# Cross-attention loops taken in turns of two pairs of chunks, with value projections and value products in runs of two pairs

## What is computed

```
x = x + cross_attention_0(layernorm(x), ctx)          # with relative positions
...
x = x + cross_attention_1(layernorm(x), ctx, mask)    # with a mask on the keys
# cross_attention: 16 heads of 16, 64 queries, 1601 keys
q = x @ Wq + bq;  k = ctx @ Wk + bk;  v = ctx @ Wv + bv
attn = softmax(scores(q, k) / 4)      # per head, over 1601 keys
out  = (attn @ v) @ Wo + bo
```

## Time and profile before

| | |
|---|---|
| median of 3 runs | 2634.69 us (2631.03 to 2641.21) |
| the profiled execution | 2644.9 us, span 2643.1 us |
| TensorE, mean granted clock | 0.962 of full speed |
| busy: TensorE | 2439.4 us (92%) |
| busy: VectorE / ScalarE / GpSimd | 1402.9 / 986.3 / 512.5 us |
| DMA | 39 GB/s mean |

### The profile page before, as it was taken

The page is one execution under the profiler, slowest core; times in us unless marked ns, Lnnn a source line. Parts: engine busy times, 40 slices in busy tenths (PEclk is TensorE's granted clock), DMA queues, the critical chain, the costliest instruction groups (busy, mean ns, idle before and its releaser), DMA issues. The chain is left out here.

```text
span 2643.1 us, 90979 instructions
## 1 busy us (share of the span) xinstructions
PE 2439.4 (92%) x41473; PEld 1761.7 (67%) x41473; DVE 1402.9 (53%) x2296; ACT 986.3 (37%) x1350; POOL 512.5 (19%) x488
## 2 busy tenths in 40 slices
PE   7999999999998888979999999999788899897898
PEld 3677776776777655647676767677567677776466
DVE  4454554455453562365545554554556666665568
ACT  2333333333332331234444444443433344333223
POOL 2322323323321212311111111110011111111000
PEclk8999999999998789989999999999899999999899
DMA  2111111111111322301111111120100000000200
GB/s 95 27 41 39 29 44 33 33 40 33 33 34 67 125 97 72 96 28 46 33 46 33 46 33 46 33 54 27 55 3 3 3 3 3 4 3 3 84 1 16
DMA packets 56727, 102.18 MB, mean 39 GB/s; under 512 B 10400, under 2 KB 49024, under 8 KB 55024
## 3 DMA queue, kind: packets, MB, share of 16 engines
q1 hardware_dynamic: 54448, 91.25, 11.3%
q0 software_dynamic: 1904, 5.15, 0.5%
HBM read 90.20 MB, written 9.21 MB: 38 GB/s over the span
## 5 line engine op out<-in xcount | busy, mean ns | idle before, releaser
L702 DVE TENSOR_REDUCE x_mx<-banks 128x2 f32<-128x800 f32 (+1 forms) x362 | 357.1, 990 | 420.0 <-PE banks L878 293.3
L903 PE MATMUL banks<-x_wv,x_cT 128*128 128x256 f32 (+1 forms) x1664 | 422.5, 396 | 4.6 <-DVE x_nmb L714 4.6
L792 PE MATMUL banks<-x_cT,x_wk 128*128 128x400 f32 (+1 forms) x1024 | 384.7, 518 | 8.0 <-DMA x_cT<-in_ctx 5.7
L903 PEld LDWEIGHTS banks<-x_wv,x_cT 128*128 128x128 f32 (+1 forms) x1664 | 296.6, 188 | 67.7 <-DVE x_nmb L714 5.8
L583 ACT ACTIVATE x_PT<-banks 128x2048 f32<-128x2048 f32 (+1 forms) x112 | 196.7, 1756 | 339.2 <-PE banks L942 339.2
L585 ACT ACTIVATE x_PT<-banks,x_kbs 128x1024 f32<-128x1024 f32 (+1 forms) x208 | 221.3, 1111 | 232.8 <-PE banks L942 232.8
L792 PEld LDWEIGHTS banks<-x_cT,x_wk 128*128 128x128 f32 x1024 | 189.1, 193 | 139.7 <-issue 26.5
L942 PE MATMUL banks<-x_qbd,x_kT 32*128 32x128 f32 x6656 | 247.6, 273 | 0.0
L942 PEld LDWEIGHTS banks<-x_qbd,x_kT 32*128 32x128 f32 x6656 | 244.0, 185 | 3.5
L922 PE MATMUL banks<-x_PT,x_V 128*32 128x64 f32 (+1 forms) x13312 | 234.5, 221 | 1.6 <-ACT x_PT L585 0.8
L922 PEld LDWEIGHTS banks<-x_PT,x_V 128*32 128x32 f32 (+1 forms) x13312 | 197.2, 110 | 49.8 <-issue 43.0
(11 more groups left out here) (411 smaller groups left out, 3631.6 us busy)
## 6 DMA issues: line engine op xcount, KB each, us to landing
x_cT<-in_ctx SPq DMA_DIRECT2D x96, 400.0 KB, 3.7
x_cT<-in_ctx SPq DMA_DIRECT2D x32, 401.0 KB, 3.9
e_up<-in_mo_up SPq DMA_DIRECT2D x9, 512.0 KB, 15.9
e_down<-in_mo_down SPq DMA_DIRECT2D x9, 512.0 KB, 15.8
x_mrow<-in_mask_row SPq DMA_DIRECT2D x1, 3202.0 KB, 14.2
t_w<-in_db_w SPq DMA_DIRECT2D x3, 1024.0 KB, 6.9
e_rows<-in_c_unfilled SPq DMA_DIRECT2D x1, 2967.0 KB, 13.6
e_xg<-e_rows SPq DMA_DIRECT2D x23, 129.0 KB, 2.1
```

The costliest lines, as they stand in the source:

```text
L702: dve.reduce_max(mx[:, H0[k]:H0[k] + 3:2, kb], g.PS[:, first:first + 2, 0:KBS[kb]], AXX).then_inc(max_read, 1)
L792: last = pe.matmul(PJ[pb][:, 0:KBS[k]], wk[:, c, gg, :], cT[:, (p + 1) % 2, c, KB0[k]:KB0[k] + KBS[k]], start=c == 0, stop=c == KC - 1)
L903: last = pe.matmul(PJ[pb][0:VCH[c + k], D * k:D * k + D], cT[:, p, cc, VK0[c + k]:VK0[c + k] + VCH[c + k]], wv[:, cc, :], start=cc == 0, s ...
```

## The change

The loops on TensorE and VectorE take two pairs at a time. For k = 0, 2, 4, 6 the order on TensorE is: a unit of maxima, scores of pair k, value projections of pairs k+1 and k+2, a unit, scores of pair k+1, a unit, value products of pairs k-1 and k. The three tables are replaced by `FRONT` (units ahead of scores), `BACK` (units behind the second scores of a turn) and `LAST` (one unit behind the loop, in the first attention only). Projections go to bank 0 for pairs 0, 2, 4, 6 and to bank 5, which the maxima also use, for pairs 1, 3, 5. A projection into bank 5 waits for the unit before it to be read, and the unit behind it waits for the copy out of bank 5. `V` holds eight chunks, and `PT` has three buffers in both attentions.

```diff
-        V = sb("V", [128, 6, H, 32])
-        NPT = 3 if rel else 2
+        V = sb("V", [128, 8, H, 32])
+        NPT = 3
...
-                self.V = [bank.use(0) for _ in range(0, NCH, 2)] if attend else None
+                self.V = [bank.use(k % 2) for k in range(NPAIR)] if attend else None
...
-        if mask:
-            SCORED = {2: 1, 4: 3, 6: 5, 8: 7, 10: 9}
-            PROJECTED = {0: 0, 2: 2, 4: 4, 6: 6, 8: 8}
-            VALUED = {}
-        else:
-            SCORED = {2: 1, 4: 3, 6: 6, 8: 8, 10: 10}
-            VALUED = {4: 4}
-            PROJECTED = {0: 0, 2: 2, 4: 5, 6: 7, 8: 9, 10: 11}
+        FRONT = {0: 0, 1: 1, 2: 3, 3: 4, 4: 6, 5: 7, 6: 9}
+        BACK = {1: 2, 3: 5, 5: 8} if mask else {1: 2, 3: 5, 5: 8, 6: 10}
+        LAST = () if mask else (11,)
...
+                if attend and ahead:
+                    maximum(FRONT[0])
                 if attend:
                     values(0)
...
-                for c in range(0, NCH, 2) if attend else ():
-                    if ahead and c in SCORED:
-                        maximum(SCORED[c])
-                    if ahead and c in VALUED:
-                        maximum(VALUED[c])
-                    if ahead and c in PROJECTED:
-                        maximum(PROJECTED[c])
-                    if c + 2 < NCH:
-                        values(c + 2)
+                for k in range(0, NPAIR, 2) if attend else ():
+                    if k and ahead:
+                        maximum(FRONT[k])
+                    for j in (k + 1, k + 2):
+                        if j < NPAIR:
+                            values(2 * j)
+                        if j == k + 1 and j in FRONT and ahead:
+                            maximum(FRONT[j])
+                    scored = min(k + 1, NPAIR - 1)
+                    if ahead and scored in BACK:
+                        maximum(BACK[scored])
+                for u in LAST if attend and ahead else ():
+                    maximum(u)
...
                     pb = take(bank, plan.V[c // 2])
+                    if pb and ahead:
+                        pe.wait_ge(max_read, units(b + 1) + FRONT[c // 2])
...
-                    for c in range(0, NCH, 2):
-                        scores(c)
-                        if ahead and c in SCORED:
-                            maximum(SCORED[c])
-                        for a in (c - 2, c - 1) if c else ():
-                            attend_values(a)
-                        if ahead and c in VALUED:
-                            maximum(VALUED[c])
-                        if c + 2 < NCH:
-                            project_values(c + 2)
-                        if ahead and c in PROJECTED:
-                            maximum(PROJECTED[c])
+                    for k in range(0, NPAIR, 2):
+                        if ahead:
+                            maximum(FRONT[k])
+                        scores(2 * k)
+                        for j in (k + 1, k + 2):
+                            if j < NPAIR:
+                                project_values(2 * j)
+                        if k + 1 < NPAIR:
+                            if ahead:
+                                pb, use = plan.V[k + 1]
+                                pe.wait_ge(free[pb], bank.value(pb, use))
+                                maximum(FRONT[k + 1])
+                            scores(2 * k + 2)
+                        scored = min(k + 1, NPAIR - 1)
+                        if ahead and scored in BACK:
+                            maximum(BACK[scored])
+                        for j in (k - 1, k):
+                            for a in (2 * j, 2 * j + 1) if 0 <= j < NPAIR - 1 else ():
+                                attend_values(a)
+                    for u in LAST if ahead else ():
+                        maximum(u)
```

More of the change, by code:

```diff
@@ L303, in __init__ @@
                 self.NM = bank.use(0) if attend else None
-                self.V = [bank.use(0) for _ in range(0, NCH, 2)] if attend else None
+                self.V = [bank.use(k % 2) for k in range(NPAIR)] if attend else None
                 self.WO = tail and not p
+        NPAIR = -(-NCH // 2)
         SECT, used = [], [0, 0, 0]
@@ L340, in next_keys @@
             return (Bank(base, stride, i - 1) if 0 < i < B // 2 - 1 else Bank(base)), plans[p], i, p
-        SCORED = {2: 1, 4: 4, 6: 7, 8: 10, 10: 13}
-        VALUED = {2: 2, 4: 5, 6: 8, 8: 11, 10: 14}
-        PROJECTED = {0: 0, 2: 3, 4: 6, 6: 9, 8: 12, 10: 15}
         H0 = [0, 1, 4, 5]
@@ L352, in cross_attention @@
         LOOPED = [(kb, k) for kb, k in ALL if (kb, k % 2) not in HEADED]
-        if mask:
-            SCORED = {2: 1, 4: 3, 6: 5, 8: 7, 10: 9}
-            PROJECTED = {0: 0, 2: 2, 4: 4, 6: 6, 8: 8}
-            VALUED = {}
-        else:
-            SCORED = {2: 1, 4: 3, 6: 6, 8: 8, 10: 10}
-            VALUED = {4: 4}
-            PROJECTED = {0: 0, 2: 2, 4: 5, 6: 7, 8: 9, 10: 11}
+        FRONT = {0: 0, 1: 1, 2: 3, 3: 4, 4: 6, 5: 7, 6: 9}
+        BACK = {1: 2, 3: 5, 5: 8} if mask else {1: 2, 3: 5, 5: 8, 6: 10}
+        LAST = () if mask else (11,)
+        assert sorted([*FRONT.values(), *BACK.values(), *LAST]) == list(range(len(LOOPED)))
         def cast(b, kb, gg=1):
@@ L724, in values @@
                     dve.wait_ge(full[pb], bank.value(pb, use))
-                    if later(b) or c >= 6:
-                        dve.wait_ge(av_done, NCH * b + (c - 4 if c >= 6 else 0))
+                    if later(b) or c >= 8:
+                        dve.wait_ge(av_done, NCH * b + (c - 6 if c >= 8 else 0))
                     if VCH[c] < VCH[min(c + 1, NCH - 1)]:
@@ L732, in values @@
                         return
-                    dve.tensor_copy(V[0:VCH[c], c % 6:c % 6 + n2, :, 0:HD],
+                    dve.tensor_copy(V[0:VCH[c], c % 8:c % 8 + n2, :, 0:HD],
                                     PJ[pb][0:VCH[c], 0:D * n2].rearrange("p (a h d) -> p a h d", a=n2, h=H)).then_inc(free[pb], 1)
+                if attend and ahead:
+                    maximum(FRONT[0])
                 if attend:
@@ L921, in attend_values @@
                         r = 32 * (h % 4)
-                        last = pe.matmul(OT[r:r + 32, S * (h // 4):S * (h // 4) + S], V[0:VCH[c], c % 6, h, :],
+                        last = pe.matmul(OT[r:r + 32, S * (h // 4):S * (h // 4) + S], V[0:VCH[c], c % 8, h, :],
                                          PT[0:VCH[c], c // 2 % NPT, c % 2, S * h:S * h + S], start=c == 0 and h < 4,
```

## The result

Four runs of the changed kernel gave 2697.91 us in the median (2684.95 to 2708.02); the kernel before, run beside it on the same chip, gave 2634.28. The ratio is 1.0214, with a 95% interval of 1.0184 to 1.0245: **slower by 2.1%**, and 39 us over the upper end of the predicted range. The profiled execution has a span of 2693.2 us, 50.1 more than the 2643.1 of before, and the mean granted clock is 0.959 (0.962 before).

What follows compares the result with a forecast made beforehand. TensorE was taken to bound both cross-attentions; +14.1 (first attention), -2.4 (second), -0.3, +1.1 and -1.8 (special batches) gave +10.7 us on 2634.7, so 2645.4 us, range 2631 to 2659.

Steps and rivals of the forecast that it cites:

- What bounds it, and the pieces: Both cross-attentions: TensorE bounds them, so the change works through its pieces' prices in their new places and its waits.
- A run of two projections: Value projections of two pairs side by side on TensorE: 3.66 us instead of 3.86.
- unit to unit: Successive units of maxima on TensorE: never under 1.43 us apart, since VectorE must read each first.
- Two pairs of value products and what leaves them: Two pairs in a run, followed by row-group work: 1.80 + 0.20 = 2.00 us.
- rival 1: Steps behind a released wait, such as value products to unit, cost more: +8 us, so 2653; chance 0.15.
- Rival 3: Each change of shape costs more than read, so fewer changes save more: -10 us, about 2635; chance 0.12.
- The new waits: TensorE waits for VectorE's reads, for exponentials in first turns, and at the first attention's loop end.
- The first turn's wait for ScalarE: Second attention, first turn: too little work covers the exponentials, so TensorE waits about 0.8 to 1 us.
- The end of the loop in the first attention: Unit 9 to the keys' projection: 4.34 us, bound by VectorE's reads, +2.48 us a batch.
- rival 4: First attention's loop end does not wait, units being read beside other work: -26 us, so 2619; chance 0.05.
- the sum in the first attention: Terms of one first-attention batch add to +1.01 us, over fourteen batches +14.1 us.
- Rival 2: Granted clock falls to half at the first attention's loop end: +12 to +24 us, about 2663; chance 0.08.

Runs made afterwards that it cites:

- e1: The changed kernel with context blocks 1 to 3 of a batch loaded only when the batch's last chunk is scored: 2673.14 us, ratio 1.0122.
- e4: The changed kernel with first-attention units 6 and 10 between the two pairs of value products, none directly ahead of the keys' projection: 2659.88 us, ratio 1.0070.
- e7: e4 with the late context loads of e1: 2646.86 us, ratio 1.0030.
- e9: The kernel before with the second attention's first value projection moved behind the first scores, directly ahead of the second's: 2636.77 us, ratio 0.9993.

## Why the prediction was wrong, step by step

The forecast was 2645.4 us, 10.7 above before; measured were 63.6.

*What bounds it, and the pieces: right.* A run of two projections takes 3.65 us (forecast 3.66) and unit to unit 1.44 (1.43), here of TensorE in the first turn of a masked batch:

```profile
1446.62 3.69 PE L905 MATMUL banks<-x_wv,x_cT 128*128 128x256 f32 x16
1450.24 0.34 PE L878 MATMUL banks<-x_kbf,x_qbf 32*128 32x400 bf16 x2
...
1453.20 0.34 PE L878 MATMUL banks<-x_kbf,x_qbf 32*128 32x400 bf16 x2
1453.91 0.40 PE L936 MATMUL banks<-x_nmb,x_ones 32*128 32x512 bf16 x4 [0.37 <-ACT x_PT L579]
...
1455.13 3.72 PE L905 MATMUL banks<-x_wv,x_cT 128*128 128x256 f32 x16
1458.78 0.34 PE L878 MATMUL banks<-x_kbf,x_qbf 32*128 32x400 bf16 x2
```

Two pairs of value products and what leaves them took 1.93 us (454.29 to 456.22) where I had 2.00; leaving them for a unit is not dearer than I took, so rival 1 is out. Rival 3's gain isn't seen either: the middle turn from L936 at 1453.91 to the next at 1462.52 is 8.61 us, against my 8.63.

*The new waits: right.* The first turn's wait for ScalarE is 0.71 us from the unit (1453.20 to 1453.91; I said 0.8 to 1). The end of the loop in the first attention, forecast at 4.34 us from unit 9 to the keys' projection:

```profile
363.88 0.34 PE L878 MATMUL banks<-x_kbf,x_qbf 32*128 32x400 bf16 x2
...
365.31 0.34 PE L878 MATMUL banks<-x_kbf,x_qbf 32*128 32x400 bf16 x2 [0.54 <-DVE x_mx L696]
...
366.75 0.34 PE L878 MATMUL banks<-x_kbf,x_qbf 32*128 32x400 bf16 x2
368.18 2.96 PE L792 MATMUL banks<-x_cT,x_wk 128*128 128x401 f32 x8 [1.09 <-DVE x_mx L696]
```

It is 4.30, and 14 x 1.09 = 15.3 us for the last wait alone against my 14 x 1.16. So rival 4 is out. Batches free of long stalls bear out the sum in the first attention: 49.15 and 50.99 us, for 48.28 and 49.83 before, +0.9 and +1.2 where I had +1.01.

*The step that failed* is none of the sum's terms but what was left out of it: "a run of two pairs costs 3.66", "two in a run ... 2.00". I priced each piece by its own rows and took for granted that TensorE is fed at any density of instructions. The rows that I took of before could not show it otherwise, since their longest stretch without a projection holds 208 instructions, less than one block. But its trace could, in the row of L2391. There, too, the gaps lie at equal distances: of the 42 the 35 over 0.3 us all leave 193 to 196 when their number is divided by 256. The densest part:

```profile
2413.81 0.21 PE L2391 MATMUL banks<-d_XX,d_C 64*64 64x64 f32 x1 [1.58 <-issue]
...
2417.68 0.21 PE L2391 MATMUL banks<-d_XX,d_Y 64*64 64x64 f32 x1 [1.35 <-issue]
```

Seven such edges follow from 2413.81 to 2437.97, one each 3.8 to 4.1 us, and from 2400 to 2443 the DMA moved nothing but ten instruction packets (4 GB/s):

```profile
q8 instruction: 10, 0.16, 1.4%
```

So TensorE got a block of 256 instructions about every 4.0 us there, with no load beside it. The new order wants 410 in a row in 5.2 us; at that pace they take 6.4 us, an estimate (410 / 256 x 4.0) that could have been made beforehand. It is an upper bound, since projections stand on either side. I looked at the lines that the change touches and not at the first row of the waits view; it named the effect, at the same kind of work. The missing term is the 33.5 us of "issue" (0.2 before), and with it part of the clock's. The Trainium skill, Runtime: NRT & Kernel Launch, section Instruction fetch mechanics, says that TensorE's instruction memory is refilled in blocks of 256 instructions of 16 KiB, and that the fetch is hidden behind the issue of instructions. The block size is what the trace shows (332 packets of 16 KB for 85,066 instructions); that it is hidden holds for the attentions of the kernel before, but neither for its L2391 nor for this one, and there the measurement decides.

*Rival 2, the falling clock, came in part.* The stretches at half clock in the two attentions sum to 34.2 us for 13.6 before, so some 10 us of work time was lost (half of the 20.6 more); I had given 12 to 24 us and a chance of 0.08. Of the seven new stretches two begin at the keys' projection behind the loop's end (261.6 and 473.2), as the rival said. The other five begin 0.2 to 1.1 us after TensorE goes on from a stall, and those are the five stalls of 2.0 us and more. Either is enough by itself: in e1, whose stalls are all under 1.2 us, six stretches begin at the loop's end and none behind a stall; in e4, without the wait at the loop's end, three begin behind its three longest stalls (1.6, 1.8 and 2.0 us); in e7, with neither, there is none but those that the kernel before has in the last batches.

*How the sum stands now.* In the two stretches read above, waits for other engines are 34 us (8 before) and "issue" 30 (0.2 before; some 4 us more lie ahead of the stretches); with gaps too short for the view they make the 58 us of idle time. Busy time fell by 6 in spite of some 10 us lost by the clock, so 16 us were saved, as I take it by the fewer changes of shape: that is a difference, and no run here isolates it. 58 - 6 = 52 us. Without stalls and clock 52 - 30 - 10 = 12 is left, where I had forecast +10.7. By attention it is 34 - 14 - 7 = 13 in the first, for 13.5 in the forecast, and 18 - 16 - 3 = -1 in the second, for -2.8. So the terms that I summed were right, and two that I had left out make up the other 40.

*The range* held rivals of known kinds alone. Nothing in it stood for the supply of instructions, which no row that I had taken showed at the new density.

## What to carry to other kernels

Gathering like pieces into longer runs saves changes of shape, but it also gathers short instructions; count instructions per microsecond between the long matmuls, and compare the longest stretch with one block of the instruction supply. If a piece stops inside a run of like matmuls, with "issue" as its releaser, look at the packets of kind "instruction" 1.2 to 1.6 us earlier, and test it by shifting the whole list by a few instructions. Read the first rows of the waits view of before even where they belong to other parts of the kernel: a limit that shows there can show where you are about to gather work. And before a wait is removed, ask which other wait ran beside it: it will be the next to end last (e9).

## What was not expected of the hardware

- TensorE stalled for 0.2 to 2.8 us inside runs of short fp32 matmuls at edges of its 256-instruction blocks, and, in the attentions of these kernels, nowhere else with "issue" as the releaser. It went on 1.2 to 1.6 us after an instruction packet had landed, in every one of the gaps over 0.9 us inside runs of scores, values' products and L936.
- A context load of 400 KB just ahead of the packet made the stall about 1 us longer: the longest gap in the scores was 2.3 us with the load and 1.0 without (e1). Without any load L2391 stalled for up to 2.0 us.
- A shift of 32 instructions moved the time from a ratio of 1.0214 to 1.0153. A dense kernel's time thus depends on the number of instructions ahead of its loop, and two such kernels can't be compared to 0.5% by one build each.
- No packet of before or after started more than 301 instructions ahead of the edge at which its block begins, and no block was used sooner than 1.2 us after its packet had landed. So hardly more than one block was on its way at a time. Why it isn't asked for earlier no run here settles.
- That it takes a stretch of more than one block was seen in few orders only (208, about 410, split, and L2391).
